# Softmax attentions: the score matmuls of the last unit, and of two heads of the last but one, issued twice by TensorE into the same bank

## What is computed

```python
q, k, v = heads(norm(x) @ Wq + bq), heads(ctx @ Wk + bk), heads(ctx @ Wv + bv)   # 16 heads of 16
attn = softmax(q @ k.T / 4)        # 512 queries x 1601 keys, for each of 4 batches and 16 heads
x = x + merge(attn @ v) @ Wo + bo
```

## Time and profile before

| | before |
|---|---|
| median of 3 runs | 3004.25 us |
| the profiled execution, its own time | 2997.46 us |
| its span, first to last instruction | 2995.5 us |
| TensorE busy | 2780.6 us (93%) |
| ScalarE busy | 1590.3 us (53%) |
| VectorE busy | 1635.9 us (55%) |
| mean granted TensorE clock | 0.934 |
| unit 15 of L0 | 733.9 to 788.5 us |
| unit 15 of L3 | 2852.7 to 2909.1 us |

### The profile page before, as it was taken

How to read it: one execution, slowest core, us unless ns; L and a number is a source line. 1 busy time by engine, 2 the same in 40 slices (tenths; PEclk the granted TensorE clock), 3 DMA queues, 4 the chain that set the end, 5 groups by cost and what they waited for, 6 DMA issues and landing times.

```text
span 2995.5 us, 38856 instructions
## 1 busy us (share of the span) xinstructions
PE 2780.6 (93%) x14660; PEld 1397.4 (47%) x14660; DVE 1635.9 (55%) x2980; ACT 1590.3 (53%) x2688; POOL 292.2 (10%) x233
## 2 busy tenths in 40 slices
PE   7999999998799898998899999979899999999877
PEld 3334344343377766776333333368633443434323
DVE  5777787775284554442112221046586777777705
ACT  1777777776300112010677878831247777777642
POOL 2010101000110101111011010031201010010000
PEclk7899999998799999999999999989979999999966
DMA  5433242330200002000734545020133423433100
GB/s 112 64 45 51 35 48 48 41 45 1 78 13 29 0 1 64 1 1 13 132 44 71 62 69 63 1 84 1 33 59 38 49 45 45 67 40 34 17 4 29
DMA packets 68951, 125.51 MB, mean 42 GB/s; under 512 B 20976, under 2 KB 45464, under 8 KB 65312
## 3 DMA queue, kind: packets, MB, share of 16 engines
q1 hardware_dynamic: 67616, 120.61, 26.2%
q10 hardware_dynamic: 1152, 2.44, 0.3%
HBM read 42.47 MB, written 2.10 MB: 15 GB/s over the span
## 4 chain that ended last, share of the span: by engine, by line
PE 56%; DVE 4%; ACT 3%; issue 2%; SPq 1%; DMA 0%; ACTq 0%; POOL 0%; POOLq 0%; DVEq 0%
PE psum L190 35%; PE psum L697 13%; PE psum L1819 6%; DVE mpart L882 2%; ACT probs L762 2%; PE psum L276 1%; PE psum L1812 0%; PE psum L707 0%; SPq L992 0%; DVE prod L1602 0%; DMA qst<-qp_lo 0%; DVE masked_hi L1906 0%; SPq L993 0%; DVE masked_lo L1907 0%; ACTq L993 0%
## 5 line engine op out<-in xcount | busy, mean ns | idle before, releaser
L762 ACT ACTIVATE probs<-psum 128x512 f32<-128x512 f32 (+3 forms) x2080 | 1282.9, 691 | 435.0 <-PE psum L190 433.3
L882 DVE TENSOR_REDUCE mpart<-psum 128x2 f32<-128x804 f32 x1024 | 976.5, 991 | 317.3 <-PE psum L190 308.2
L697 PE MATMUL psum<-probs,vt 128*17 128x512 f32 (+1 forms) x4992 | 683.3, 623 | 0.4 <-ACT probs L762 0.3
L190 PE MATMUL psum<-qst,kst 50*128 50x512 f32 (+3 forms) x2496 | 624.8, 461 | 39.2 <-ACT probs L762 34.2
L190 PEld LDWEIGHTS psum<-qst,kst 50*128 50x128 f32 (+3 forms) x2496 | 275.4, 188 | 464.5 <-issue 309.6
L190 PE MATMUL psum<-kst,qst 48*128 48x402 f32 x2048 | 415.6, 428 | 48.7 <-DVE mpart L882 46.6
L190 PEld LDWEIGHTS psum<-kst,qst 48*128 48x128 f32 x2048 | 197.8, 195 | 359.7 <-issue 184.9
L190 PE MATMUL psum<-wv,ctxT 128*128 128x256 f32 (+1 forms) x624 | 181.4, 419 | 1.5 <-DVE kp_lo L863 0.5
L190 PE MATMUL psum<-ctxT,wk 128*128 128x512 f32 (+1 forms) x384 | 159.7, 546 | 22.5 <-DMA ctxT<-in_ctxT 21.3
L697 PEld LDWEIGHTS psum<-probs,vt 128*17 128x17 f32 (+1 forms) x4992 | 85.3, 96 | 202.8 <-issue 164.4
L190 PEld LDWEIGHTS psum<-wv,ctxT 128*128 128x128 f32 (+1 forms) x624 | 109.6, 194 | 77.4 <-issue 58.6
(11 more groups left out here) (281 smaller groups left out, 2749.1 us busy)
## 6 DMA issues: line engine op xcount, KB each, us to landing
kst<-kp_hi SPq DMA_DIRECT2D x144, 200.1 KB, 5.9
ctxT<-in_ctxT SPq DMA_DIRECT2D x36, 512.0 KB, 5.6
kst<-kp_lo SPq DMA_DIRECT2D x72, 200.1 KB, 5.4
qst<-qp_hi SPq DMA_DIRECT2D x144, 64.0 KB, 4.5
kst<-kp_hi SPq DMA_DIRECT2D x84, 100.1 KB, 2.9
qst<-qp_lo SPq DMA_DIRECT2D x72, 64.0 KB, 5.1
kst<-kp_lo SPq DMA_DIRECT2D x42, 100.1 KB, 3.0
stage<-in_L_ffn_W SPq DMA_DIRECT2D x16, 256.0 KB, 4.5
```

Of the source, the lines that this page charges most:

```text
L190: last = e.matmul(dst, lhsT, rhs, start=i == 0, stop=i == len(pairs) - 1)
L697: t = e.matmul(c.bank(self.acc)[32 * h:32 * h + VW, :], self.vt[0:kn, kc, self.head(g, h), :], p[0:kn, h % self.wide, :], start=kc == 0, s ...
L762: e.activation(self.probs[n % slots][0:kn, :, :], c.psum[0:kn, k:k + self.wide, :], ACT.Exp if softmax else ACT.Sigmoid, scale=DH ** -0.5) ...
L882: e.tensor_reduce(self.mpart[:, :, p * (SEQ // P) + qt, i], c.psum[:, k:k + 2, 0:MAX_WIDTH], AX.X, ALU.max).then_inc(c.drained(k), 1)
```

## The change

A scores step for which the new `twice` is true loops over the head h0 two times. `self.wide` is 1 in a softmax attention, so `h - h0` is 0 in both rounds: the same weights (keys) and the same moving data (queries) go twice into the same bank, each a matmul of its own that begins and ends its accumulation. Only the second one signals `filled`. The steps are all 52 of unit 15, and heads 0 and 1 of unit 14 (26 steps), in both softmax attentions. Nothing else changes: no wait, no bank, no order.

```diff
     def behind_maxima(self, step):
         return self.softmax and step[2:4] >= (UNITS - 2, 10)
+
+    def twice(self, step):
+
+        _, _, u, _, h0 = step
+        return self.softmax and (u == UNITS - 1 or u == UNITS - 2 and h0 < 2)
...
-                for h in range(h0, h0 + self.wide):
+                for h in range(h0, h0 + self.wide) if not self.twice(step) else (h0, h0):
                     at = slice(64 * (h % 2), 64 * (h % 2) + rows)
                     t = mm(e, c.bank(k + h - h0)[0:kn, :], [(self.kst[u % 3][at, h // 2, k0:k0 + kn],
                                                              self.qst[u % 3][at, h // 2, :])])
```

## The result

| | before | after |
|---|---|---|
| median | 3004.49 us (6 runs, 3000.99 to 3009.49) | 3027.40 us (6 runs, 3020.02 to 3035.63) |
| ratio, 95% interval | | 1.0075 (1.0055 to 1.0095) |
| profiled execution, its own time | 2997.46 us | 3024.09 us |
| span | 2995.5 us | 3022.1 us |
| mean granted TensorE clock | 0.934 | 0.933 |

A forecast was written before the change was run, and what follows sets the result against it. TensorE, busy 93%, was taken to bound the kernel. Unit 15 (+5.9, +4.1) and unit 14 (-0.4, -1.2) summed to +8.4 us on 3004.25, say 3013 us; own range 3002 to 3022, wide range 2990 to 3030.

The forecast's parts named there:

- the stop: Unit 15, waits ahead of banks 5 and 7: both stay, TensorE idle over a microsecond at each.
- the wide range: Whole kernel's time: 2990 to 3030 us, less than 2 in 10 outside.
- rival B: Units 14 and 15: clock as before, every added matmul paid; +27 and +3 to +6 us, 3033; chance 0.13.
- Price of a twin: Units 14 and 15: each added score matmul costs 0.23 us at the upper clock level, 0.40 at the lower.
- ScalarE's start behind a stop: Unit 15: ScalarE starts 0.74 us after the first matmul following the wait, instead of 0.51.
- The ring: Unit 15, each seven scores: 5.46 to 6.4 us at the upper clock, 8.0 to 10.2 at the lower.
- the pv: Unit 15, matmul among the scores, 1.75 per seven: pushed two steps, 0.46 us upper clock; 1.4 lower for all.
- The clock in unit 15: Unit 15: half the time at the upper level, unit 60.5 us; +5.9 us in L0, +4.1 in L3.
- Unit 14: Unit 14: 26 added matmuls cost +3.0 us, clock returns -2.6 and -4.2; net -0.4 and -1.2.
- What follows unit 15 only begins later: Blocks behind unit 15: they start later, with no cost of their own in the sum.
- A: Units 14 and 15: added matmuls keep the clock at 2.4 GHz almost throughout; -15 us, 2989; chance 0.20.
- C: Units 14 and 15: added matmuls nearly free as ScalarE paces; within 5 us of 3000; chance 0.20.

The follow-up runs named there:

- no_stop: Kernel before, nothing added, the wait ahead of banks 5 and 7 asks for one visit fewer: 2943.26 us against 3005.28, ratio 0.9786.
- early_twin: Changed kernel's added matmuls, the first of each two issued ahead of the wait: 3002.69 us against 3005.96 for the kernel before, ratio 0.9989.

## Why the prediction was right, and where it was off

- *Direction and mechanism.* The forecast was 3013 us, up 8.4, with slower the likeliest case. The reason given is what the runs show: a twin stands behind the stop, on the path, and leaves the stop where it is.
- *The size.* The measured 22.9 us are 2.7 times the 8.4. 3027.4 lies within the wide range, but outside the 3002 to 3022 that the forecast gave itself, and nearer to rival B's 3033 than to 3013: that it lies in the range at all is owed to the room left for B, which is luck as far as the forecast's own sum goes.
- *Two slips in the sums.* By its own terms unit 14 of L0 is +3.0 - 2.6 = +0.4, not -0.4, so the forecast's sum is +9.2 and not +8.4. B's terms, +27 and +3 to +6, give 3034 to 3037, not 3033. Neither changes the reasoning.
- *Price of a twin.* Predicted 0.23 us at the upper clock and 0.40 at the lower; measured 0.23 (0.73 against 0.50) and 0.43 (1.23 against 0.80). ScalarE's start behind a stop: predicted 0.74 us, measured 0.74 and 0.72.
- *The ring.* Predicted 6.4 and 10.2 us, measured 6.14 and 9.7. At the upper clock the two stops cost 0.23 each, as taken, but the pv only one step more and not two: ScalarE idles 0.65 us behind it where it idled 0.41. At the lower clock the pv costs 0.85, two steps, as taken.
- *The clock in unit 15.* I took half of the unit at the upper level; over eight units it was 0.36, from 0.14 to 0.48. In the profile of the timed comparison it was 0.48, and there the unit came out at 59.8 us against 60.5 predicted; but that was a lucky draw. With 0.36 and the measured rings the same sum gives 1/(0.36/6.14 + 0.64/9.7) = 8.0 us a ring and 61.6 us a unit; the traces have 62.9. This term was mis-sized: +10.0 predicted for both attentions, +13.7 measured.
- *Unit 14.* Predicted -1.6 in all (-0.8 with the slip put right), measured -5.9 in the traces. The upper level is held nearly throughout (0.96 to 1.00); how much of this is twins that cost less than I took and how much is clock was not separated.
- *The step that failed.* "What follows unit 15 only begins later" priced the blocks behind at nothing. They meet a clock that falls earlier, and that is +3.4 us behind L0 and +3.8 behind L3.
- *The sum.* 13.7 - 5.9 + 3.4 + 3.8 = +15.0 us, and the means of the spans in the table differ by 15.9. The timed runs say 22.9, at least 16.5. The traced executions before took 3004.3 us on average, as the timed ones; those after took 3020.1, 7 us less than the timed median. The rest of the distance therefore lies between the four traces after and the six timed runs. By their mean clocks and spans (an estimate) the timed ones spent 418 us at the lower level and the traced ones 395. In which part isn't shown, and whether it is more than luck stays open.
- *Rivals.* A (the twins hold the clock up) came true for unit 14 and not for unit 15: 0.36 instead of 0.20 is a rise that doesn't pay for the rings. B had unit 15 at +14 and +13 with an unchanged share; the pair at 0.57 and 0.58 shows +11.5, and four of the eight units after had a clock of 0.57 to 0.66, near B's 0.6. C is refuted by 0.74 us at a stop and by the ring of 6.14 us, where C wanted less than 5.8.
- *The rules of the pages.* The rule cited for the forecast, that gaps between groups of matmuls from cycling through PSUM banks make the clock swing (the Trainium skill, "TensorE: Matmul & The Clock Gate", section "A second HAM failure mode: psum-queue depth-cycling"), agrees with no_stop: with the stops gone and no matmul added the clock goes from 0.62 and 0.60 to 0.84 and 0.94. But the run shortens the unit as well, so TensorE is busy for 0.89 and 0.88 of it where it was 0.76 and 0.75, and whether the gaps or the busy share does it is not separated. The rule cited beside rival A, to keep TensorE busy without a break (the Trainium skill, same page, section "Why this matters for your kernels"), is not met by twins in unit 15: there TensorE is busy for 0.77 of the time in the profile after, hardly more than before, and stops as often.

## What to carry to other kernels

In this kernel, work added to keep TensorE's clock up shortened a unit only where little of it was on the path. Where an engine restarts behind a wait, put such work ahead of the wait (early_twin, 25 us better than the changed kernel with the same matmuls), and first ask whether the wait is needed: one visit fewer in one wait was worth 62 us. And where the clock is drawn anew in each execution, two profiles are not enough to price a part; unit 15 of one and the same kernel ranged over 8 us.

## What was not expected of the hardware

- A score matmul of 128 columns in front of one of 512 on the same rows of the array delays its end by 0.21 us at the lower clock (1.01 against 0.80 for two pairs), half of what a full one of 512 does (0.43).
- Identical instructions took 2795.9 to 2821.4 us outside the four units in seven traces of two kernels. Where the traces drift apart, stretches at 1.2 GHz mostly lie in different places.
- The state in which the clock is left goes with the length of the next block: the 172 VectorE instructions behind L3 took 85.8 to 86.6 us where the upper level lasted 11.3 us or more into them, and 89.0 to 91.8 where it lasted at most 4.5, in thirteen traces of eight kernels.
